# Cross-attention keys and values from seven half-depth products of summed operands, against twelve-matmul direct products

## Time and profile before

| | |
|---|---|
| median of 3 runs | 900.28 us (900.24 to 901.11) |
| the profiled execution's own time | 900.3 us |
| its span, first to last instruction | 898.5 us |
| TensorE busy | 885.5 us (99%) |
| VectorE, ACT, GpSimd busy | 596.1 us (66%), 464.4 us (52%), 204.8 us (23%) |
| mean granted TensorE clock | 0.997 of full |
| chain that ended last | 96% TensorE |
| the 48 steps | 393.2 to 673 us from the span's start |

### The profile page before, as it was taken

One profiled execution on the slowest core, in us unless ns is written; L12 is line 12 of the kernel. 1 busy time (PEld: TensorE's weight loads), 2 busy tenths in 40 slices (PEclk: granted clock), 3 DMA queues, 4 the chain that ended last, 5 costly groups with the idle time before them and its releaser, 6 DMA issues.

```text
span 898.5 us, 17919 instructions
## 1 busy us (share of the span) xinstructions
PE 885.5 (99%) x7088; PEld 778.1 (87%) x7088; DVE 596.1 (66%) x1304; ACT 464.4 (52%) x1119; POOL 204.8 (23%) x147
## 2 busy tenths in 40 slices
PE   8999999999999999999999999999999999999995
PEld 8998989898989899877788888888877898999994
DVE  7886566666666635675665656646557878888883
ACT  5543333333333344547766666666675336656551
POOL 0143232323232215301101111011000621132233
PEclk9999999999999999999999999999999999999998
DMA  6221242424212115040200001000043688989973
GB/s 225 66 94 42 78 141 80 138 84 135 85 64 90 47 47 181 28 137 1 84 24 25 13 24 37 13 24 14 1 167 123 243 303 302 358 283 305 297 206 47
DMA packets 42195, 104.56 MB, mean 116 GB/s; under 512 B 8208, under 2 KB 18560, under 8 KB 40192
## 3 DMA queue, kind: packets, MB, share of 16 engines
q1 hardware_dynamic: 37808, 94.23, 30.7%
q0 software_dynamic: 4304, 9.19, 5.0%
HBM read 75.57 MB, written 18.65 MB: 105 GB/s over the span
## 4 chain that ended last, share of the span: by engine, by line
PE 96%; DVE 2%; ACT 0%; issue 0%; DMA 0%; POOL 0%; DVEq 0%
PE bank L595 25%; PE bank L596 24%; PE bank L597 24%; PE bank L852 5%; PE bank L869 5%; PE bank L695 3%; PE bank L671 3%; PE bank L683 1%; PE bank L711 1%; PE bank L812 1%; PE bank L981 1%; PE bank L879 1%; PE bank L989 1%; DVE pp L1745 0%; PE bank L819 0%
## 5 line engine op out<-in xcount | busy, mean ns | idle before, releaser
L1380 ACT ACTIVATE ee<-bank 125x448 f32<-125x448 f32 x192 | 90.8, 546 | 13.6 <-PE bank L852 13.6
L1628 DVE TENSOR_TENSOR E_lo<-F,E_hi 128x940 fp32r<-128x940 f32 (+3 forms) x62 | 80.8, 1320 | 2.2 <-ACT E_hi L1147 2.1
L595 PE MATMUL bank<-wkv_hi,ctx_hi 128*125 128x512 f32 x192 | 79.9, 416 | 0.0
L2330 POOL TENSOR_TENSOR ctx_lo<-ctx_f,ctx_hi 128x500 fp32r<-128x500 f32 x24 | 30.6, 1276 | 204.2 <-ACT ctx_hi L1147 204.2
L596 PE MATMUL bank<-wkv_hi,ctx_lo 128*125 128x512 f32 x192 | 76.2, 397 | 0.0
L597 PE MATMUL bank<-wkv_lo,ctx_hi 128*125 128x512 f32 x192 | 75.8, 395 | 0.0
L1147 ACT ACTIVATE E_hi<-F 128x940 fp32r<-128x940 f32 (+3 forms) x62 | 67.9, 1140 | 7.9 <-PE bank L597 3.6
L2330 POOL TENSOR_TENSOR wqk_lo<-wqk_f,wqk_hi 128x1024 fp32r<-128x1024 f32 x14 | 35.1, 2507 | 155.5 <-ACT wqk_hi L1147 155.5
L2440 POOL DMA_INDIRECT out<-yg,meta x21 | 39.5, 1880 | 126.1 <-DMA out<-yg,meta 72.1
L595 PE MATMUL bank<-wv_hi,xT_hi 128*128 128x256 f32 x224 | 63.5, 283 | 0.1
L597 PE MATMUL bank<-wv_lo,xT_hi 128*128 128x256 f32 x224 | 62.6, 279 | 0.0
(11 more groups left out here) (411 smaller groups left out, 2571.3 us busy)
## 6 DMA issues: line engine op xcount, KB each, us to landing
F<-wexp SPq DMA_DIRECT2D x14, 1408.0 KB, 7.7
F<-wexp SPq DMA_DIRECT2D x14, 768.0 KB, 6.9
wqk_f<-wqk SPq DMA_DIRECT2D x16, 512.0 KB, 4.3
ctx_f<-ctx SPq DMA_DIRECT2D x24, 250.0 KB, 2.8
slots<-zt SPq DMA_DIRECT2D x3, 1799.0 KB, 8.1
xg<-slots SPq DMA_DIRECT2D x21, 256.0 KB, 7.4
wv_f<-wv SPq DMA_DIRECT2D x8, 512.0 KB, 5.5
wo_f<-wo SPq DMA_DIRECT2D x8, 512.0 KB, 3.5
```

Source lines behind the costliest of these rows:

```text
L595: e.matmul(out, a[0], b[0], start=first, stop=False)
L1380: e.activation(ee[(4 * n + r) % 8][:, :], SX[r][0:MS, 0:4 * T], ACT.Exp, scale=0.25).then_inc(*x_exped.did((n, r)))
L1628: return e.tensor_tensor(out, src, high.bitcast(F32), ALU.subtract)
L2330: return e.tensor_tensor(out, src, high.bitcast(F32), ALU.subtract)
```

## The change

Context tiles 0 to 5 (batches 0 and 1, steps 0 to 11; `NPL = 12`) are computed as before. Tiles 6 to 23 are taken in 9 pairs c, each with both halves `hf`: 18 pair jobs k. For one k, two context tiles (rows) by two depth halves times two depth halves by two column halves (values, keys) is a 2 x 2 block product, done with seven products of depth 256 and 256 columns (the Winograd form of Strassen), each 2 depth chunks x 3 matmuls 128x256. So 42 matmuls of 256 columns replace 24 of 512. Sums of products are done partly by accumulation in a PSUM bank, partly on VectorE.

```
+CROSS = (1, 6, 7, 5, 2, 4, 3)
...
+        in_step, z = {n: [] for n in range(NK)}, 0
+        for n, k in enumerate([5, 4, 3, 4, 5, 5] + [4, 3] * 13 + [2, 2, 3, 2]):
+            in_step[NPL - 4 + n] = products[z:z + k]
...
+            def cross_pe(k, i):
...
+                if i == 1 and k:
+                    w.wait_ge(*v1_kept[k - 1])
...
+                elif i == 7:
+                    w.wait_ge(*(pair_sum[k - 1, 3] if k else kn_done[items[-1]]))
+                elif i == 2:
+                    w.wait_ge(*pair_sum[k, 6])
+                elif i == 4:
+                    w.wait_ge(*pair_sum[k, 5])
+                new = i in (1, 7)
+                for j in range(2):
+                    for x, y in ((0, 0), (1, 0), (0, 1)):
+                        t = e.matmul(PX[i], a[x][:, j, :], b[j][y], start=new and j + x + y == 0, stop=j == 1 and y == 1, skip_group_check=True)
```

```
+        t_order, t_sums, x_sums = (1, 3, 2, 4), (3, 1, 2, 4), (5, 6, 3, 7)
+        t_step = {n: [(t_order[n % 4], n // 4)] for n in range(2, 8)}
+        t_step[1] = [(t_order[0], 0), (t_order[1], 0)]
+        x_step = {4: [(0, 1), (0, 6), (0, 7)], 5: [(0, i) for i in (5,) + other_x], 6: [(1, 1)], 7: [(1, 6), (1, 7), (1, 5)],
+                  8: [(1, i) for i in other_x]}
...
+            def weight_hi(i, hf):
+
+                w.wait_ge(*t_set[i, hf])
+                if i > 1:
+                    w.wait_ge(*t_set[{2: 4, 3: 2, 4: 4}[i], hf])
+                hi(TW[i][0][:, :, hf, :], t_f[f"{i}lo"][:, :, hf, :]).then_inc(*t_hi.did((i, hf)))
+
+            def context_hi(c, i):
+
+                if i in x_sums:
+                    w.wait_ge(*x_set[c, i])
...
             def step(n):
...
+                for it in t_step.get(n, []):
+                    weight_hi(*it)
                 for k in ctx_step.get(n, []):
                     ctx_hi_act(k)
-                if n + 4 < NK:
+                for it in x_step.get(n, []):
+                    context_hi(*it)
+                if n + 4 < NPL:
                     rows_square(*keys[n + 4])
...
+                for k, j in in_step[n]:
+                    if j == 6:
+                        first_keep(k)
+                    if j == 2:
+                        value_rows(k)
```

The GpSimd list becomes:

```
+            for i in t_sums:
+                weight_sum(i, 0)
+            weight_low(1, 0)
+            weight_low(3, 0)
+            ctx_low(4)
+            weight_low(2, 0)
+            ctx_low(5)
+            weight_low(4, 0)
+            context_sums(0)
+            for i in t_sums:
+                weight_sum(i, 1)
+            for i in CROSS:
+                context_low(0, i)
+            for i in t_order:
+                weight_low(i, 1)
+            for c in range(1, NCP):
+                context_sums(c)
+                for i in CROSS:
+                    context_low(c, i)
```

```
+            w.wait_ge(*wqx_lo[1])
+            quarter_load("1hi", 0, toks(256, 256))
+            quarter_load("1lo", 0, toks(0, 256))
             rows_load(range(NA))
             w.wait_ge(*pj_full["o", NH // 2 - 1, NA - 1])
             e.dma_start(gw_f[:, :, :], gw_d).then_inc(*gw_in.did(0))
+            for b in range(NB):
+                w.wait_ge(*rows_in[b][len(row_parts[b]) - 1])
+            quarter_load("3hi", 2, toks(0, 256))
+            quarter_load("2hi", 2, toks(256, 256))
...
-        s_step = {3: [(0, 0)], 4: [(0, 1)], 5: [(0, 2)], NK - 4: [(1, 0), (1, 1), (1, 2)], NK - 3: [(2, 0), (2, 1), (2, 2)],
-                  NK - 2: [(3, 0), (3, 1), (3, 2)]}
+        s_step = {43: [(0, 0), (0, 1)], 44: [(0, 2), (1, 0)], 45: [(1, 1), (1, 2)], 46: [(2, 0), (2, 1), (2, 2)],
+                  47: [(3, 0), (3, 1), (3, 2)]}
```

More of the change, by code:

```diff
@@ L236, in decoder_layer @@
         half = sbl("half", [128, 2], F32, "free")
+        ssp, rrp, rqp = (sbl(n, [MS, 2 * XH], F32, "free") for n in ("ssp", "rrp", "rqp"))
         zz = sbl("zz", [T, XH, 16], F32, "wv")
@@ L342, in decoder_layer @@
         items = keys[:4] + [(0, "q")]
-        for n in range(NK):
-            items += keys[n + 4:n + 5] + ([(n // MC + 1, "q")] if n % MC == 0 and n // MC + 1 < NU else [])
+        for n in range(NPL - 4):
+            items += [keys[n + 4]] + ([(n // MC + 1, "q")] if n % MC == 0 else [])
+        assert len(items) == NPL + NPX and (NPX - 1, "q") == items[-2]
         at_item = {it: n for n, it in enumerate(items)}
@@ L354, in aside, with pair_items @@
             return (("n", 3, b - 1) if i == 2 else ("g", b - 1, i + 1)) if b else None
+        pairs = [(MC * z + c, hf) for z in range(NCP // MC) for c, hf in ((0, 0), (1, 0), (0, 1), (1, 1), (2, 0), (2, 1))]
+        NPR = len(pairs)
+        last_pair = {c: max(k for k in range(NPR) if pairs[k][0] == c) for c in range(NCP)}
+        def pair_items(k):
+            c, hf = pairs[k]
+            return [6 * (t // MC) + MC * hf + t % MC for t in (6 + 2 * c, 7 + 2 * c)]
+        products = [(k, i) for k in range(NPR) for i in CROSS]
@@ new lines, in decoder_layer, with value_step, homes @@
+        pair_of, q_after = {}, {}
+        for k in range(NPR):
+            for a, n in enumerate(pair_items(k)):
+                pair_of[n] = k, a
+                assert done_step[k] + 3 <= n
+            for u in q_step:
+                if prod_step[k, 2] == q_step[u]:
+                    q_after[k] = u
+        def value_step(n):
+            return n + 1 if n % MC == 1 else n
+        def homes(lives):
+            until, home, before = [], {}, {}
+            for a, b, n in sorted(lives):
+                free = [i for i in range(len(until)) if until[i][0] < a]
+                i = min(free, key=lambda i: until[i]) if free else len(until)
+                if not free:
+                    until.append(None)
+                home[n], before[n] = i, until[i][1] if free else None
+                until[i] = b, n
+            return home, before, len(until)
@@ L508, in decoder_layer @@
         gw_hi, gw_lo = sig("gw_hi", [0]), sig("gw_lo", [0])
[L509 to L513, removed]
+        ctx_step = {2: [4], 3: [5]}
@@ L1400, in step @@
                 x, i = aside(n), n % 6
-                new = [keys[n + 3]] if 0 < n and n + 3 < NK else []
-                if m == 1 and u + 1 < NU:
+                new = [keys[n + 3]] if 0 < n and n + 3 < NPL else []
+                if m == 1 and u + 1 < NPX:
                     new += [(u + 1, "q")]
```

495 lines of the change are left out of this document (417 added, 78 removed).

## The result

The changed kernel takes **952.2 us** (951.3 to 953.8, 4 runs) against 900.6 (900.2 to 901.1, 4 runs): ratio **1.0575**, 95% interval 1.0556 to 1.0593, 51.7 us slower. I had forecast 906.3, 894 to 913. The sign was right and the size wrong by a factor of nine.

The account below looks back on a forecast made before the run. TensorE, busy 99% of the span, was taken as the bound, every wait in its list paid in full. Terms -11.0 + 3.4 + 3.1 + 2.9 + 4.0 + 1.7 + 0.8 + 0.3 + 0.8 = +6.0 gave 906.3 us, range 894 to 913.

Parts of the forecast that it names:

- Products -11.0: TensorE, 18 pair jobs: 42 matmuls of 256 columns replace 24 of 512, saving 0.61 us each, 11.0 us.
- splits +3.4: TensorE: pair turns between two products pay the change of matmul kind, 18 splits at 0.19 us, +3.4 us.
- The three waits of the preparation, +10.0: Steps 1, 4 and 7: ACT's hi parts wait for GpSimd's sums, delaying TensorE's turns by 3.1, 2.9 and 4.0 us.
- the landing: Step 1: last row copy lands 2.2 us after issue near 395.5, last quarters land at 404.0 (402.5 to 405.7).
- Waits inside the pairs, +1.7 and +0.8: Product 2 waits in steps 8 and 13 (+0.6, +1.1); pair's turn late after queries in steps 19, 25, 31, 37 (+0.8).
- Costed at nothing: VectorE's 23 us more, ACT's added splits, later row copies and late shared-expert weight loads were taken to cost no time.
- The tail, +0.3: Steps 43 to 47: three more splits for ACT and VectorE cost 0.3 us (0 to 4).
- GpSimd against VectorE, +0.8: GpSimd's added operations hold small VectorE operations, 0.3 us at each of three preparation waits, +0.8 us (0 to 10).
- The third rival: VectorE is held by GpSimd in every pair: +9 us on the forecast, 915 us; chance 0.11.
- Weight loads as the bound (0.01): Rival: 18 more weight loads per job, each standing free at 0.1 us or more, add 32 us: 938; chance 0.01.

Follow-up runs that it names:

- run 12: Run 11 with weight sums and weight lo parts made by VectorE, where its list waits for TensorE's rows, not by GpSimd: 901.0 us, ratio 1.0002.
- run 3: The changed kernel with the pair's turn (key transposes and their copies) behind the step's last product instead of its second: 941.9 us, ratio 1.0459.
- run 6: Changed kernel with preparation and end reordered, pair's turn behind the last product, plus queries' turn in its own step and new VectorE/ACT list places: 918.8 us.
- run 7: Run 6 with the pair's turn placed step by step and third-norm rows behind the pair's additions in VectorE's list: 910.2 us, ratio 1.0098.
- 11: Run 7 with the order of VectorE's and ACT's lists changed and the pair's turn of step 30 last: 906.1 us, ratio 1.0055.
- run 9: The changed kernel with 18 filler matmuls of 64 columns ahead of the pair's turn in steps 14, 20, 26, 32, 38: 957.9 us, ratio 1.0620.

## Why the prediction was right or wrong

**Where the 51 us are.** From the three stages: idle 10.3 + 31.1 + 4.1 = 45.5. Half clock, by TensorE's busy time against run 12, whose granted clock is 1.00 in all three: 48.0 - 45.5, 211.9 - 204.8, 18.5 - 16.5, together 11.5. The saving, 274.2 - 266.8 = 7.4. 45.5 + 11.5 - 7.4 = 49.6, of a difference of 51.0 in the spans; 1.2 of the rest lie ahead of step 0, where kernels with the same list there differ by as much.

**Products -11.0, splits +3.4: right.** Run 12 takes 7.9 less of TensorE in steps 8 to 43, where the two terms made 7.6. A split costs what I took: in steps 18, 24, 30 and 36 the products and the pair's turn take 3.62 with the turn in their middle (after) and 3.45 with it behind them (run 3), idle time left out, so 0.17 against 0.19. That the sum is so close is in part luck. Counted from start to start against the kernel before, products and queries lose 6.2 to the change of kind, not 3.4, since they stand in more blocks, and the transposes, whose number stays, take 10.0 in place of 13.4 (a pair's four take 0.35 ahead of products, where two took 0.31 ahead of values).

**The three waits of the preparation, +10.0: right in place, short in size.** Measured idle before the turns 4.8, 3.2 and 4.2 against 3.1, 2.9 and 4.0. The chains are the ones that I named: ACT's hi part waited 4.8 and 3.6 for a weight sum of GpSimd ahead of the first two waits, 2.9 and 1.1 for context sums ahead of the third. The first was the worst, and its failed step is the landing: the last row copy was issued at 397.1 and landed 4.5 later, at 401.6, not 2.2 later at 397.7, so the last quarters landed at 407.3, beyond my bound of 405.7. (The 2.2 was read from a copy of 32 KB; the last one has 224 KB.) I had also put the later copies at nothing. The gate weights come behind them: ACT waited 1.4 for these, the keys behind it came late, and a row product of step 1 waited 1.3. What I left out altogether is what follows a wait: steps 0 to 7 lost 12.8 and step 8 seven, with a half-clock stretch in steps 2 and 8.

**Waits inside the pairs, +1.7 and +0.8: over-sized.** Products waited 0.5 in all for VectorE's additions (in step 13). That is in part luck: with the turn ahead of it moved or mended, the same product waited 3.6 (run 3) and 2.2 (run 6).

**"Costed at nothing": the step that failed.** It said that VectorE's added load is "covered by TensorE", since its share stays at 71%. A share says nothing of when an operation is wanted. The products take all four half banks of banks 0 and 1, so the queries' turn had to move to bank 7, beside the pair's and the one put aside; each waits until VectorE has read the one before, and VectorE reads them in a list where scalings and additions stand ahead. I had written that no idle time of more than 0.5 would stand between steps 14 and 43; there are waits of 0.5 to 2.2 in 16 of these 30 steps, and the steps took 16.6 more where I had some 5 less. Runs 3, 6, 7 and 11 changed nothing but places and order and took back 10.4, 6.8, 8.6 and 4.1 (part of it in steps 8 to 13). How much of this is the one bank and how much the order of VectorE's and ACT's lists, no run separates. The bank was told in the diff; I priced the transposes and never asked who empties what they write to.

**The tail, +0.3: wrong, 6.6, beyond its bound of 4.** Step 44's norm turn waited 4.1 for the copy of queries that stood behind shared weights in VectorE's list, then it ran at half clock (0.50 from 699.0 to 705.7): the same error.

**GpSimd against VectorE, +0.8, bounds 0 to 10: under-sized.** I took 0.3 at each of the three waits; on the first chain two small operations lasted 0.62 and 1.19 in place of 0.17, on the second three lasted 0.53 to 0.55. Taking the weights off GpSimd, with room in VectorE's list, brought 5.1 (run 12 against 11), 4.3 of them in steps 0 to 7. The Trainium skill, SBUF — State Buffer, section "Who interferes with whom", has the two engines lock each other out of a shared port for a whole instruction; the trace agrees, in both directions: GpSimd's 0.63 for a context sum became 1.70 when VectorE made its sums. The third rival put that hold into every pair as the main loss, 9 us. It is real there too (step 18 of run 12 has a scaling of 1.17 in place of 0.69) but small: in steps 14 to 43 of after the pairs' 45 small operations and 15 scalings lasted together 1.5 more than at their shortest. With the weights' 5.1, the hold is the lesser part of what was lost.

**The clock.** My price of a wait was its length. In after, six of the nine waits of 2 us or more (steps 2, 8, 26, 32, 38 and 44) were followed by a stretch at half clock, a quarter more on top of all idle time (11.5 on 45.5), and 8 fillers in a hole took three such stretches away. The Trainium skill, TensorE: Matmul & The Clock Gate, section "Part 1: The HAM clock gate", names idle time as what brings the lower level; the trace agrees there. The other three (steps 5, 13 and 20: 3.2, 2.5 and 2.2) kept full clock, and in run 9 the same wait of step 13 was followed by half clock (0.50 from 500.1 to 503.4). What decides it is open.

**Weight loads as the bound (0.01): excluded**, the products are 0.119 apart.

## What to carry to other kernels

When a change takes a spare buffer away, list for each one that is left its writers in order, who empties it, and what stands ahead of that reader in its engine's list; only then call an engine's added work covered. In a kernel in which one engine is never idle, price a wait at more than its length, and put a row of extra work on the engine that has room *at that moment*, not in the mean. Small edits of place and order, and of which engine makes the weight sums, were worth 51 us here, more than the arithmetic could ever bring.

## What the runs showed of the hardware that I had not expected

- Adding matmuls to an idle time made the kernel 3.5 us faster: behind 2.15 us of idle time the granted clock was 0.57 over 4 us; with the same place filled, the products behind it ran 0.12 apart.
- A plain float32 matmul of 64 columns shows as two records and took 0.22 to 0.24 (18 took 4.0, 8 took 1.9), as long as a matmul of 512 columns in the split products; I had counted half of that.
- VectorE's operation on 125x16 numbers takes 0.17 to 0.2, and in several places 1.0 to 1.2 while a GpSimd operation on tiles in SBUF ran; GpSimd's own operation went from 0.63 to 1.70 the other way.
- The last row copy (224 KB) landed 4.5 us after issue where 1 MB of quarters and the 13 other copies had been issued in the 10 us ahead of it, and 2.7 us in the kernel before, where the copies alone were spread over 15 us.
